# Attention over key tiles: one block of products per tile, four score banks, three single maxima banks

## The chip, the cores and the metric

The kernel runs on 1 core of one Trainium2 chip. The metric is the time of one execution in device microseconds (us); three runs were taken of the kernel before. The core's engines are named as in the profile: PE (TensorE, with its weight loads shown apart as PEld), DVE (VectorE), ACT (ScalarE), POOL (GpSimd) and SP (SyncE, which issues DMAs). Matmul results land in PSUM, eight banks of 128 partitions by 512 f32 numbers.

## The reference, cut to what matters

The whole reference is two transformer layers over 4096 tokens of width 256. The change touches the attention of the first layer alone: 16 heads of 16 numbers, every token against every token, with a bias linear in the distance.

```python
score = jnp.einsum('bhsd,bhnd->bhsn', q, k) / scale + bias[None]
attn = jax.nn.softmax(score, axis=-1)
out = jnp.einsum('bhsn,bhnd->bhsd', attn, v)
```

Behind it come a mixture of 64 experts, a second attention and a gated linear attention, each with its own stage in the kernel; they are the same in both versions.

## The kernel before, in words

`bias_attention` (from L663) walks over 8 chunks of 512 queries (c) and, in each, over 4 groups of 4 heads (g): 32 steps, each of 32 key tiles of 128 keys (k). A key tile makes three kinds of work.

- **Scores** (`score`, L1163 to L1171): for each of the 4 heads one matmul of 54 rows gives keys by queries, 128 x 512, into one of three banks `ps_exp`. ACT takes the exponential of each bank (`exps`, L831 to L837) into `probs`, which has two buffers of four heads.
- **Maxima**: the softmax needs each query's largest score before its exponentials are taken, so a step ahead of the scores PE makes the same products the other way round, queries by keys, for the *next* step (`unit_half`, L1139 to L1156). A unit is a pair of heads for 128 queries and 512 keys, two matmuls of 128 x 512; 64 units make a step, two go with each key tile. A unit fills a buffer of two banks, `ps_max0` or `ps_max1` in turn, and DVE reads the pair in one reduction of 128 x 1024 to 128 x 2 (L1100 in `units`). At the end of a step a short chain of DVE operations (L907 to L924) joins the maxima.
- **Products** (`products`, L1173 to L1188): probabilities times values, into one bank `ps_out`, four heads side by side in column groups of 32. They run one key tile behind the scores.

A score or a maxima matmul uses 54 of the array's rows, in its upper or lower half; one of each stand next to each other in PE's order, in opposite halves, and run side by side. A product uses all 128 rows and 32 columns, four heads side by side.

The order on PE is written by hand in `step` (L1217 on): for each half q of a key tile two scores and the two halves of one unit in turn, then the products of half the queries (256 columns).

```python
for q in range(2):
    for h in range(2):
        score(c, g, k, 2 * q + h)
        if ahead:
            mm = unit_half(c, g, d, u + q, 1 - h)
    ...
        products(c, g, k - 1, q)
```

The waits that matter: a unit's matmul waits until DVE has read the unit two before (semaphore `unit_read`, L1151); a score waits for the exponential three before (`exp_done`, L1169); the products of a tile wait for its four exponentials (L1177). The first 72 units (one step and 8 units) run before the first score. In the last step there is no unit to make, and in the step before it none for the last 4 tiles.

From the second chunk on, six pieces of the routing of the chunk before (`extra`, L1190 to L1215: transposes, router logits, ranks) are inserted on PE per chunk, behind the products of the tiles listed in EXTRA. Each takes one maxima buffer in turn, and ACT copies it out (L844 to L867). DVE's small operations of the routing stand between its reads of units (`pieces`, L1075). SP loads keys and values by counts of scores and products done (L739 to L754); POOL clears rows by counts of units read (L784).

Of the kernel before, what the change touches and what calls it, by code (L numbers as in the profile page):

```python
# [377 lines left out]
EB = 3  # L378
ROWS = 2 * NPR * BIAS * TC
EXPS = NT * HG  # L380
assert UNITS == 2 * NT and AHEAD % 2 == 0 and (NG * EXPS + 1) % EB == 0 and ROWS == P // 4
# [240 lines left out]
def extras_ahead(g, u):  # L622

    return sum(1 for xg, xk in EXTRA if xg < g or xg == g and unit_at(xk) < u)


def unit_place(c, g, d, u):

    ahead = g + d - 1
    if isinstance(c, int) and NG * c + ahead < 0:  # L630
        return u
    block, row = c + ahead // NG, ahead % NG
    place = UNITS * (NG * c + g + d) + u
    if isinstance(block, int) and block == 0:
        return place
    return place + len(EXTRA) * (block - 1) + extras_ahead(row, u)


def extra_place(c, i):

    g, k = EXTRA[i]
    return UNITS * (NG * c + g + 1) + unit_at(k) + 1 + len(EXTRA) * (c - 1) + i


def extra_behind(c, g, d, u, back):

    ahead = g + d - 1
    for i, (xg, xk) in enumerate(EXTRA):
        if c + ahead // NG >= 1 and xg == ahead % NG and unit_at(xk) + back == u:
            return i  # L650
    return None


def extra_buffer(i):

    return (unit_at(EXTRA[i][1]) + 1 + i) % 2
# [6 lines left out]
def bias_attention(nc, q_laid, k_laid, m_rows, v_aug, x_rows, y_rows, hT_rows, xres, mod, ident, r, slots, w_router, e_bias):  # L663

    with ExitStack() as ctx:
# [11 lines left out]
        ps_max = [pb(f"ps_max{i}", [P, 2, CH]) for i in range(2)]  # L677
# [19 lines left out]
        summed = lambda c, i: extra_place(c, i) + 1  # L697
        read = lambda c, i: len(EXTRA) * (c - 1) + i + 1

        with nc.Block() as block:  # L700
            @block.sync
            def _(sp):
# [34 lines left out]
                def step(c, g, last):  # L737

                    s = NG * c + g  # L739
                    for b in range(4):  # L740
# [6 lines left out]
                        if not (last and g == NG - 1):  # L747

                            hold(sp, pv_done, 2 * (NT * s + (b + 1) * QUART + 2), sp_passed)
                            load_vals((g + 1) % NG, b)  # L750
# [24 lines left out]
            def _(pool):  # L775
# [7 lines left out]
                for b in range(SLOTS // step_rows):  # L783
                    pool.wait_ge(unit_read, 2 + UNITS + 16 * (b + 1))  # L784
                    pool.dma_start(x_rows[b * step_rows:(b + 1) * step_rows, :].rearrange("(p r) d -> p r d", p=P),
                                   zeros[:, :].unsqueeze(1).to_broadcast([P, CLEAR_ROWS, PAY])).then_inc(cleared, 16)
# [43 lines left out]
            def _(act):  # L830
                def exps(s, g, k):  # L831

                    act.wait_ge(pv_done, 2 * (NT * s + k + 1))
# [5 lines left out]
                def copy_o(s, g):  # L839

                    act.wait_ge(pv_done, 2 * (NT * (s + 1) + 2))
                    act.activation(r.o[g][:, :], ps_out[:, :], ACT.Copy).then_inc(o_copied, 1)  # L842

                def copy_heads(c, i):  # L844
                    act.wait_ge(unit_summed, summed(c, HEADS + i))
                    act.wait_ge(heads_set, c - 1)
                    for half_ in range(2):
                        ps = ps_max[extra_buffer(HEADS + i)][:, half_, :].rearrange("p (h w) -> p h w", h=H0)
# [3 lines left out]
                def copy_turned(c, k):  # L852
                    act.wait_ge(unit_summed, summed(c, TURN + k))
                    act.activation(r.turned()[:, k, :], ps_max[extra_buffer(TURN + k)][:, 0, :],
                                   ACT.Copy).then_inc(extra_read, 1)

                def router_exp(c):
# [3 lines left out]
                                   ps_max[extra_buffer(LOGITS)][:, 0, 0:TC * E], ACT.Exp, scale=-1.0).then_inc(extra_read, 1)  # L861

                def copy_ranks(c):
# [3 lines left out]
                                   ps_max[extra_buffer(RANKS)][:, 0, :], ACT.Copy).then_inc(extra_read, 1)  # L867
# [33 lines left out]
            def _(dve):  # L901
# [3 lines left out]
                def maxima(s, i):  # L905
                    dve.wait_ge(unit_read, 2 + UNITS * (s + 1))
# [183 lines left out]
                def units(c, g, d, behind=True, first=False, link=None, span=range(UNITS)):  # L1090
# [3 lines left out]
                    for u in span:  # L1094
                        kb, row = divmod(u, TC * NPR)
                        tile, pair = divmod(row, NPR)
                        place = unit_place(c, g, d, u)
                        buffer = (u + (extras_ahead((g + d - 1) % NG, u) if link is not None else 0)) % 2
# [34 lines left out]
            def _(pe):  # L1133

                pe.sem_inc(unit_read, 2)
                pe.sem_inc(pv_done, 4)
                pe.sem_inc(exp_done, 2)

                def unit_half(c, g, d, u, h):  # L1139
# [8 lines left out]
                    place = unit_place(c, g, d, u)  # L1148
                    buffer = (u + extras_ahead((at - 1) % NG, u)) % 2 if not isinstance(place, int) else place % 2
                    behind, before_last = (extra_behind(c, g, d, u, back) for back in (1, 2))  # L1150
                    pe.wait_ge(unit_read, UNITS * (NG * c + at) + u + (1 if behind is None else 2))  # L1151
                    if before_last is not None:
                        pe.wait_ge(extra_read, read(c, before_last))
                    mm = pe.matmul(ps_max[buffer][:, h, :], quer[at % NG][half(h), pair, tile * P:(tile + 1) * P],  # L1154
                                   keys[at % 2][half(h), pair, kb * CH:(kb + 1) * CH], start=True, stop=True)
                    return mm  # L1156

                def unit(c, g, d, u):
                    for h in range(2):
                        mm = unit_half(c, g, d, u, h)  # L1160
                    mm.then_inc(unit_summed, 1)

                def score(c, g, k, j):  # L1163
# [5 lines left out]
                    pe.wait_ge(exp_done, EXPS * s + (n + 1 if g == 0 and n < 2 else n))  # L1169
# [3 lines left out]
                def products(c, g, k, q):  # L1173

                    s = NG * c + g
                    if q == 0:
                        pe.wait_ge(exp_done, EXPS * s + HG * (k + 1) + 2)  # L1177
                        if k % QUART == 0:
                            pe.wait_ge(v_loaded[k // QUART], 16 * (s + 1))
                        if k == 0:  # L1180

                            pe.wait_ge(o_copied, s)
# [1718 lines left out]
```

## Time and profile before

| what | value |
|---|---|
| median of 3 runs | 5146.05 us (5146.01 to 5150.23) |
| the profiled execution | 5163.93 us, span 5162.3 us |
| mean granted TensorE clock | 0.953 of full speed |
| PE busy | 4681.8 us, 91% of the span |
| DVE busy | 4057.1 us, 79% |
| ACT busy | 3071.8 us, 60% |
| POOL busy | 1114.2 us, 22% |

Every duration below is from that one profiled execution, which took 17.9 us more than the median. "Busy" is time in which at least one instruction of the engine was under way; matmuls are pipelined and their ends are modelled, so a busy PE is not PE at its peak, and two instructions that overlap count once. Weight loads (PEld) run beside the matmuls. In a timeline, a row that starts a little before the one ahead of it has ended is an overlap on the same engine.

### The profile page before, as it was taken

To read this page: it belongs to the slowest core of one execution; us is meant where nothing else is said; L and a number is where in the kernel's file an instruction comes from. 1 tells how busy PE (TensorE), PEld (TensorE's weight loads), DVE (VectorE), ACT (ScalarE), POOL (GpSimd) and SP (SyncE) were. 2 spreads that over 40 slices of the span, in tenths; PEclk is the share of its full clock that TensorE was granted. 3 is DMA by queue.
4 is the path that set the end of the run, shared out by engine and by line. 5 is a ranking of instruction groups with operands and counts; after the bars stand their busy time and mean duration, and the time that the engine had idled before them with its cause. 6 is when DMAs were issued, how large, how long until landed. Compare 5 with 4: busy or idle time off the path is not lost. (4 is left out here: it accounts for less than half of the span.)

```text
span 5162.3 us, 101254 instructions
## 1 busy us (share of the span) xinstructions
PE 4681.8 (91%) x39032; PEld 2403.0 (47%) x39032; DVE 4057.1 (79%) x5031; ACT 3071.8 (60%) x5309; POOL 1114.2 (22%) x1152
## 2 busy tenths in 40 slices
PE   5589999999999999999999888547899969999998
PEld 3233333333333333333333456425566646666666
DVE  4499999999999999999998233377765448788787
ACT  1158888888888888888888512112222225555554
POOL 0000012102121021211212210254320004444443
PEclk8679999999999999999999989879999979999999
DMA  5736545354443534444342137632110031111010
GB/s 181 165 87 156 137 75 114 67 90 90 80 81 71 89 72 89 78 75 85 67 86 53 33 107 224 202 95 79 60 55 4 11 125 31 28 27 29 25 29 17
DMA packets 242778, 421.66 MB, mean 82 GB/s; under 512 B 42569, under 2 KB 147034, under 8 KB 242256
## 3 DMA queue, kind: packets, MB, share of 16 engines
q1 hardware_dynamic: 195504, 341.87, 30.1%
q0 software_dynamic: 30048, 66.76, 4.1%
q10 hardware_dynamic: 16896, 8.39, 0.7%
q8 instruction: 236, 3.87, 0.3%
q14 instruction: 94, 0.77, 0.1%
HBM read 324.51 MB, written 129.17 MB: 88 GB/s over the span
## 5 line engine op out<-in xcount | busy, mean ns | idle before, releaser
L1100 DVE TENSOR_REDUCE attn_mpart<-attn_ps_max 128x2 f32<-128x1024 f32 x2048 | 2450.0, 1221 | 100.6 <-PE attn_ps_max L1154 95.0
L837 ACT ACTIVATE attn_probs<-attn_ps_exp 128x512 f32<-128x512 f32 x4096 | 2226.7, 595 | 315.0 <-PE attn_ps_exp L1170 231.4
L1154 PE MATMUL attn_ps_max<-attn_keys,attn_quer 54*128 54x512 f32 x4096 | 1481.4, 458 | 69.9 <-DMA attn_keys<-k_laid 37.9
L1170 PE MATMUL attn_ps_exp<-attn_quer,attn_keys 54*128 54x512 f32 x4096 | 1504.2, 447 | 0.2 <-ACT attn_probs L837 0.2
L1185 PE MATMUL attn_ps_out<-attn_probs,attn_vals 128*32 128x256 f32 x16384 | 1310.1, 391 | 9.8 <-ACT route_o L842 9.2
L1170 PEld LDWEIGHTS attn_ps_exp<-attn_quer,attn_keys 54*128 54x128 f32 x4096 | 616.2, 185 | 836.2 <-ACT attn_probs L837 781.4
L1185 PEld LDWEIGHTS attn_ps_out<-attn_probs,attn_vals 128*32 128x32 f32 x16384 | 323.4, 108 | 750.3 <-issue 394.9
L1154 PEld LDWEIGHTS attn_ps_max<-attn_keys,attn_quer 54*128 54x128 f32 x4096 | 591.7, 188 | 119.3 <-DVE attn_mpart L1100 75.9
L1724 POOL DMA_INDIRECT ra_rows<-y_rows,slots x256 | 252.8, 987 | 300.8 <-DVE ra_total L1892 227.0
L577 POOL DMA_INDIRECT x_rows<-route_pay,route_now x256 | 252.0, 984 | 299.9 <-DMA x_rows<-route_pay,route_now 213.0
L1856 ACT ACTIVATE ra_row<-ra_psS 128x512 f32<-128x512 f32 x112 | 66.9, 597 | 360.9 <-PE ra_psS L1777 360.9
L1796 PE MATMUL ra_psO<-ra_vals,ra_probT 128*128 128x256 f32 x1056 | 256.5, 388 | 7.8 <-DVE ra_probT L1972 7.8
L2379 POOL TENSOR_TENSOR gla_ke<-gla_kg,emask 128x512 f32<-128x512 f32 x128 | 152.2, 1217 | 514.7 <-DVE gla_kg L2605 514.7
L1777 PE MATMUL ra_psS<-ra_kT,ra_qT 128*128 128x512 f32 (+3 forms) x576 | 240.7, 573 | 6.6 <-DVE ra_kT L1942 6.6
L1796 PEld LDWEIGHTS ra_psO<-ra_vals,ra_probT 128*128 128x128 f32 x1056 | 198.9, 196 | 42.4 <-DVE ra_probT L1972 10.0
L2670 PE MATMUL gla_psP<-gla_wqkv,gla_hc 128*128 128x512 f32 x384 | 189.7, 631 | 2.5 <-ACT gla_egn L2459 2.0
L2464 ACT ACTIVATE gla_sq<-gla_psO 128x512 f32<-128x512 f32 x32 | 19.1, 597 | 266.4 <-PE gla_psO L2778 266.4
L2365 POOL TENSOR_TENSOR gla_qeT<-gla_ftT,gla_emr 128x512 f32<-128x512 f32 x128 | 173.1, 1385 | 14.0 <-ACT gla_ftT L2411 14.0
L1777 PEld LDWEIGHTS ra_psS<-ra_kT,ra_qT 128*128 128x128 f32 x576 | 109.2, 197 | 124.8 <-issue 114.3
L1594 DVE TENSOR_TENSOR exp_hidden<-exp_psU,exp_gate 128x256 f32<-128x256 f32 x64 | 27.2, 425 | 174.0 <-PE exp_psY L1647 144.1
L1972 DVE COPY ra_probT<-ra_psT 128x512 f32<-128x512 f32 (+2 forms) x144 | 90.2, 644 | 84.6 <-PE ra_psT L1787 83.7
L1892 DVE TENSOR_REDUCE ra_total<-ra_rows 128x256 f32<-128x2048 f32 x32 | 116.9, 3653 | 39.7 <-DMA ra_rows<-y_rows,slots 39.7
(390 smaller groups left out, 5346.8 us busy)
## 6 DMA issues: line engine op xcount, KB each, us to landing
attn_keys<-k_laid SPq DMA_DIRECT2D x256, 256.0 KB
attn_vals<-v_aug SPq DMA_DIRECT2D x128, 512.0 KB, 7.7
attn_keys<-k_laid SPq DMA_DIRECT2D x256, 128.0 KB
x_rows<-attn_zeros POOLq DMA_DIRECT2D x16, 1280.0 KB, 6.2
exp_x<-x_rows SPq DMA_DIRECT2D x64, 320.0 KB
exp_w1w<-in_w SPq DMA_DIRECT2D x64, 256.0 KB
y_rows<-exp_y SPq DMA_DIRECT2D x64, 256.0 KB
attn_keys<-k_laid SPq DMA_DIRECT2D x256, 48.0 KB
```

The source lines that it names most:

```text
L577: pool.indirect_dma_start(out=x_rows, out_offset=bass.IndirectOffsetOnAxis(ap=r.now[:, n, k:k + 1].bitcast(U32), axis=0), in_=r.pay[:, n, ...
L837: act.activation(probs[k % 2][:, j, :], ps_exp[bank_of(g, n)][:, :], ACT.Exp).then_inc(exp_done, 1)
L1100: dve.tensor_reduce(mpart[i][:, kb, TC * pair + tile::TC * NPR], ps_max[buffer][:, :, :], AX, ALU.max).then_inc(unit_read, 1)
L1154: mm = pe.matmul(ps_max[buffer][:, h, :], quer[at % NG][half(h), pair, tile * P:(tile + 1) * P], keys[at % 2][half(h), pair, kb * CH:(kb + ...
L1170: pe.matmul(ps_exp[bank_of(g, n)][:, :], keys[g % 2][half(h), pair, k * P:(k + 1) * P], quer[g][half(h), pair, :], start=True, stop=True). ...
L1185: mm = pe.matmul(ps_out[j * VW:(j + 1) * VW, n], vals[:, k, j * VW:(j + 1) * VW], probs[k % 2][:, j, n], start=(k == 0 and q == 0), stop=( ...
L1724: pool.indirect_dma_start(out=rows[n % 2][:, k, :], out_offset=None, in_=y_rows, in_offset=bass.IndirectOffsetOnAxis(ap=slots[:, n, k:k + ...
L1777: mm = pe.matmul(psS[g % 2][:, 0:width], qT[s // TC % 2][:, k, s % TC * P:(s % TC + 1) * P], kT[:, k, b * BLK:b * BLK + width], start=(k = ...
L1796: mm = pe.matmul(psO[s % 2][:, :], probT[(before(s) + b) % 2][:, j * P:(j + 1) * P], vals[:, n, :], start=(n == 0), stop=(n == s))
L2365: last = pool.tensor_tensor(qeT[:, b, :, :], ftT[:, 3, b, :].unsqueeze(1).to_broadcast([P, NE, P]), emr[i][:, :, :], ALU.mult)
L2379: last = pool.tensor_tensor(ke[i][:, e, :], kg2[:, :], emask[:, bass.ds(m, 1), e].to_broadcast([P, KDV]), ALU.mult)
L2670: mm = pe.matmul(ps, hc[i][:, k, :], wqkv[:, x, k, :], start=(k == 0), stop=(k == KD - 1))
```

## The change

All of it is in `bias_attention` and its helpers.

- The products of a key tile are one block of four matmuls of 512 columns behind all four scores and both units, in place of two blocks of four of 256 columns.
- The score banks become four (EB = 4), and a score waits for the exponential four before.
- The maxima's two buffers of two banks become a ring of three single banks (MB = 3). Each half of a unit takes the next bank, has its own count on `unit_summed` and `unit_read`, and DVE reads it alone: 128 x 512 to 128 x 1, twice as many reductions. A half waits until the half three places before has been read. The number of PSUM banks stays eight (3 + 4 + 1 for 4 + 3 + 1).
- A routing insert takes one or two places of the ring (two for the heads' transposes).

```diff
-EB = 3
+EB = 4
...
+EXTRA_BANKS = (2, 2, 1, 1, 1, 1)
+MB = 3
...
+def half_number(at, u, q):
+
+    return 2 * (UNITS * at + u) + q
+
+
+def half_place(at, u, q):
+
+    return half_number(at, u, q) + extras_before(at, u)[1]
...
-        ps_max = [pb(f"ps_max{i}", [P, 2, CH]) for i in range(2)]
+        ps_max = [pb(f"ps_max{i}", [P, CH]) for i in range(MB)]
...
-                        dve.wait_ge(unit_summed, place + 1)
-                        dve.tensor_reduce(mpart[i][:, kb, TC * pair + tile::TC * NPR], ps_max[buffer][:, :, :], AX,
-                                          ALU.max).then_inc(unit_read, 1)
+                        for q in range(2):
+                            dve.wait_ge(unit_summed, half_number(s, u, q) + extras_before(s, u)[0] + 1)
+                            at = TC * pair + tile + (1 - q) * TC * NPR
+                            dve.tensor_reduce(mpart[i][:, kb, at:at + 1], ps_max[half_place(s, u, q) % MB][:, :], AX,
+                                              ALU.max).then_inc(unit_read, 1)
...
+                def bank_free(place):
+                    if place - MB in EXTRA_PLACES:
+                        pe.wait_ge(extra_read, read(*EXTRA_PLACES[place - MB]))
+                    elif place >= MB:
+                        pe.wait_ge(unit_read, PLACES[place - MB] + 1)
...
-                    pe.wait_ge(unit_read, UNITS * (NG * c + at) + u + (1 if behind is None else 2))
...
-                    mm = pe.matmul(ps_max[buffer][:, h, :], quer[at % NG][half(h), pair, tile * P:(tile + 1) * P],
+                    place = half_place(NG * c + at, u, 1 - h)
+                    bank_free(place)
+                    mm = pe.matmul(ps_max[place % MB][:, :], quer[at % NG][half(h), pair, tile * P:(tile + 1) * P],
                                    keys[at % 2][half(h), pair, kb * CH:(kb + 1) * CH], start=True, stop=True)
-                    return mm
+                    mm.then_inc(unit_summed, 1)
...
-                    pe.wait_ge(exp_done, EXPS * s + (n + 1 if g == 0 and n < 2 else n))
+                    pe.wait_ge(exp_done, EXPS * s + n)
...
-                    n = slice(q * CH // 2, (q + 1) * CH // 2)
                     for j in range(HG):
-                        mm = pe.matmul(ps_out[j * VW:(j + 1) * VW, n], vals[:, k, j * VW:(j + 1) * VW],
-                                       probs[k % 2][:, j, n], start=(k == 0 and q == 0),
-                                       stop=(k == NT - 1 and q == 1), skip_group_check=True)
+                        mm = pe.matmul(ps_out[j * VW:(j + 1) * VW, :], vals[:, k, j * VW:(j + 1) * VW],
+                                       probs[k % 2][:, j, :], start=(k == 0), stop=(k == NT - 1), skip_group_check=True)
                     mm.then_inc(pv_done, 1)
...
-                        for q in range(2):
-                            for h in range(2):
-                                score(c, g, k, 2 * q + h)
-                                if ahead:
-                                    mm = unit_half(c, g, d, u + q, 1 - h)
...
+                        score(c, g, k, 0)
+                        if ahead:
+                            unit_half(c, g, d, u, 1)
+                        score(c, g, k, 1)
+                        if ahead:
+                            unit_half(c, g, d, u, 0)
+                        score(c, g, k, 2)
+                        if ahead:
+                            unit_half(c, g, d, u + 1, 1)
+                        score(c, g, k, 3)
+                        if ahead:
+                            unit_half(c, g, d, u + 1, 0)
+                        if k >= 1:
+                            products(c, g, k - 1)
```

The order on PE before, in the first chunk's second step: one key tile. `ps_exp` are score banks (L1170), `ps_max` the maxima's buffers of two banks (L1154), `ps_out` the products (L1185); the digits are buffer numbers.

```order
L1170 MATMUL attn_ps_exp1<-attn_quer1,attn_keys1 128x512
L1154 MATMUL attn_ps_max1<-attn_keys0,attn_quer2 128x512
L1170 MATMUL attn_ps_exp2<-attn_quer1,attn_keys1 128x512
L1154 MATMUL attn_ps_max1<-attn_keys0,attn_quer2 128x512
L1185 MATMUL attn_ps_out<-attn_probs1,attn_vals 32x256 x4
L1170 MATMUL attn_ps_exp0<-attn_quer1,attn_keys1 128x512
L1154 MATMUL attn_ps_max0<-attn_keys0,attn_quer2 128x512
L1170 MATMUL attn_ps_exp1<-attn_quer1,attn_keys1 128x512
L1154 MATMUL attn_ps_max0<-attn_keys0,attn_quer2 128x512
L1185 MATMUL attn_ps_out<-attn_probs1,attn_vals 32x256 x4
```

Each unit fills both banks of one buffer, and a block of products stands between any two units.

The order on PE with the change, at a key tile of the first chunk's third step (scores are now L1164, maxima L1149, products L1177; `ps_max0` to `ps_max2` are single banks).

```order
L1177 MATMUL attn_ps_out<-attn_probs1,attn_vals 32x512 x4
L1164 MATMUL attn_ps_exp0<-attn_quer2,attn_keys0 128x512
L1149 MATMUL attn_ps_max2<-attn_keys1,attn_quer3 128x512
L1164 MATMUL attn_ps_exp1<-attn_quer2,attn_keys0 128x512
L1149 MATMUL attn_ps_max0<-attn_keys1,attn_quer3 128x512
L1164 MATMUL attn_ps_exp2<-attn_quer2,attn_keys0 128x512
L1149 MATMUL attn_ps_max1<-attn_keys1,attn_quer3 128x512
L1164 MATMUL attn_ps_exp3<-attn_quer2,attn_keys0 128x512
L1149 MATMUL attn_ps_max2<-attn_keys1,attn_quer3 128x512
L1177 MATMUL attn_ps_out<-attn_probs0,attn_vals 32x512 x4
```

Between two blocks of products the first and the fourth maxima matmul now take the same bank, here `ps_max2`.

On DVE, before, reads of the two buffers alternate; with the change the reads walk through the three banks.

```order
L1094 TENSOR_REDUCE attn_mpart0<-attn_ps_max1 128x1
L1094 TENSOR_REDUCE attn_mpart0<-attn_ps_max2 128x1
L1094 TENSOR_REDUCE attn_mpart0<-attn_ps_max0 128x1
L1094 TENSOR_REDUCE attn_mpart0<-attn_ps_max1 128x1
L1094 TENSOR_REDUCE attn_mpart0<-attn_ps_max2 128x1
```

Each row is a reduction of one bank to one column, where L1100 took two banks to two columns.

## Rows read from the trace of the kernel before

**Rows 1.** Busy time by stretch: us, engines' busy us (instructions), granted clock, DMA.

```profile
222.00:302.00 80.00, 55.53 (x142) 20.45 (x140) 79.44 (x74) 0.00 (x0) 0.00 (x0) 0.50 0.59 105
303.00:2907.00 2604.00, 2586.83 (x24728) 979.24 (x24728) 2452.26 (x2494) 2260.46 (x4184) 428.67 (x472) 1.00 0.44 85
2835.00:2903.00 68.00, 67.44 (x608) 25.89 (x607) 0.00 (x0) 64.64 (x122) 15.69 (x16) 1.00 0.04 10
3000.00:3100.00 100.00, 78.33 (x298) 58.03 (x297) 29.34 (x70) 16.72 (x33) 0.72 (x1) 0.86 0.44 138
```

The engines' columns are, in this order, PE, PEld, DVE, ACT and POOL.

**Rows 2.** Groups by line: busy us, mean ns of one, idle before, its releaser.

```profile
L1100 DVE TENSOR_REDUCE attn_mpart<-attn_ps_max 128x2 f32<-128x1024 f32 x2048 | 2450.0, 1221 | 100.6 <-PE attn_ps_max L1154 95.0
L837 ACT ACTIVATE attn_probs<-attn_ps_exp 128x512 f32<-128x512 f32 x4096 | 2226.7, 595 | 315.0 <-PE attn_ps_exp L1170 231.4
...
L1170 PE MATMUL attn_ps_exp<-attn_quer,attn_keys 54*128 54x512 f32 x4096 | 1504.2, 447 | 0.2 <-ACT attn_probs L837 0.2
L1185 PE MATMUL attn_ps_out<-attn_probs,attn_vals 128*32 128x256 f32 x16384 | 1310.1, 391 | 9.8 <-ACT route_o L842 9.2
...
L1154 PEld LDWEIGHTS attn_ps_max<-attn_keys,attn_quer 54*128 54x128 f32 x4096 | 591.7, 188 | 119.3 <-DVE attn_mpart L1100 75.9
```

**Rows 3.** Timeline of the weight loads: start us, us, engine, line, operation, idle.

```profile
1499.64 0.18 PEld L1170 LDWEIGHTS attn_ps_exp<-attn_quer,attn_keys 54*128 54x128 f32 x1 [0.41 <-ACT attn_probs L837]
...
1500.87 0.18 PEld L1170 LDWEIGHTS attn_ps_exp<-attn_quer,attn_keys 54*128 54x128 f32 x1 [0.41 <-ACT attn_probs L837]
...
1501.54 0.16 PEld L1185 LDWEIGHTS attn_ps_out<-attn_probs,attn_vals 128*32 128x32 f32 x8 [0.37 <-issue]
1502.11 0.18 PEld L1170 LDWEIGHTS attn_ps_exp<-attn_quer,attn_keys 54*128 54x128 f32 x1 [0.41 <-ACT attn_probs L837]
...
1514.44 0.18 PEld L1170 LDWEIGHTS attn_ps_exp<-attn_quer,attn_keys 54*128 54x128 f32 x1 [0.41 <-ACT attn_probs L837]
```

**Rows 4.** Timeline of PE's matmuls in the same half tile.

```profile
1500.88 0.50 PE L1170 MATMUL attn_ps_exp<-attn_quer,attn_keys 54*128 54x512 f32 x1
...
1501.21 0.39 PE L1154 MATMUL attn_ps_max<-attn_keys,attn_quer 54*128 54x512 f32 x1
1501.22 0.39 PE L1170 MATMUL attn_ps_exp<-attn_quer,attn_keys 54*128 54x512 f32 x1
```

**Rows 5.** Timeline of DVE where a small operation stands between two reads.

```profile
819.41 1.23 DVE L1100 TENSOR_REDUCE attn_mpart<-attn_ps_max 128x2 f32<-128x1024 f32 x1 [0.86 <-PE attn_ps_max L1154]
820.55 0.16 DVE L1048 TENSOR_SCALAR route_wsum<-route_wsum 128x4 f32<-128x4 f32 x1
820.64 1.23 DVE L1100 TENSOR_REDUCE attn_mpart<-attn_ps_max 128x2 f32<-128x1024 f32 x1
```

**Rows 6.** Timeline of ACT and DVE in the half tile of rows 4.

```profile
1501.41 0.60 ACT L837 ACTIVATE attn_probs<-attn_ps_exp 128x512 f32<-128x512 f32 x1
...
1501.90 0.59 ACT L837 ACTIVATE attn_probs<-attn_ps_exp 128x512 f32<-128x512 f32 x1
...
1501.68 1.23 DVE L1100 TENSOR_REDUCE attn_mpart<-attn_ps_max 128x2 f32<-128x1024 f32 x1
```

**Rows 7.** Groups by line and shape: f32 matmuls of 256 and of 512 columns.

```profile
L1796 PE MATMUL ra_psO<-ra_vals,ra_probT 128*128 128x256 f32 x1056 | 256.5, 388 | 7.8 <-DVE ra_probT L1972 7.8
L1777 PE MATMUL ra_psS<-ra_kT,ra_qT 128*128 128x512 f32 x480 | 216.6, 605 | 6.6 <-DVE ra_kT L1942 6.6
```

**Rows 8.** DVE on 512 elements from PSUM: a group, and a timeline.

```profile
L2526 DVE TENSOR_REDUCE gla_kmx<-gla_psP 128x8 f32<-128x512 f32 x32 | 22.1, 692 | 65.5 <-PE gla_psP L2674 65.5
...
4252.76 0.69 DVE L2599 SCALAR_TENSOR_TENSOR gla_qg<-gla_psP,gla_eg 128x512 f32<-128x512 f32 x1 [0.95 <-PE gla_psP L2670]
4253.37 0.68 DVE L2605 TENSOR_TENSOR gla_kg<-gla_kx,gla_egn 128x512 f32<-128x512 f32 x1
```

**Rows 9.** Timeline in the prologue: a read, and the load that waited for it.

```profile
254.17 1.21 DVE L1100 TENSOR_REDUCE attn_mpart<-attn_ps_max 128x2 f32<-128x1024 f32 x1
...
255.44 0.29 PEld L1154 LDWEIGHTS attn_ps_max<-attn_keys,attn_quer 54*128 54x128 f32 x2 [0.84 <-DVE attn_mpart L1100]
```

More of the change, by code:

```diff
@@ L619, in unit_at, with extras_before, extra_place @@
     return AHEAD + 2 * k + 1
[L622 to L639, printed above, removed]
-    g, k = EXTRA[i]
[L642 to L656, printed above, removed]
+EXTRA_BANKS = (2, 2, 1, 1, 1, 1)
+MB = 3
+def extras_before(at, u):
+    done = [i for c in range(1, NC) for i, (g, k) in enumerate(EXTRA) if (NG * c + g + 1, unit_at(k)) < (at, u)]
+    return len(done), sum(EXTRA_BANKS[i] for i in done)
+def half_number(at, u, q):
+    return 2 * (UNITS * at + u) + q
+def half_place(at, u, q):
+    return half_number(at, u, q) + extras_before(at, u)[1]
+def extra_place(c, i, b):
+    g, k = EXTRA[i]
+    return half_place(NG * c + g + 1, unit_at(k), 1) + 1 + b
+PLACES = {half_place(at, u, q): half_number(at, u, q) for at in range(NG * NC) for u in range(UNITS) for q in range(2)}
+EXTRA_PLACES = {extra_place(c, i, b): (c, i) for c in range(1, NC) for i in range(len(EXTRA)) for b in range(EXTRA_BANKS[i])}
 DVE_LINKS, POOL_LINKS = 18, 19
@@ L1212, in extra @@
                         pe.wait_ge(mask_set, c)
[L1213 to L1214 removed]
+                        pe.matmul(ps[0][:, 0:TC * E], r.prior[:, :], r.maskb[:, :, :], start=True, stop=True)
+                        mm = pe.matmul(ps[0][:, TC * E:2 * TC * E], r.onesb[:, :], r.maskb[:, :, :], start=True, stop=True)
                     mm.then_inc(unit_summed, 1)
@@ L1224, in step @@
                         u %= UNITS
-                        for q in range(2):
-                            for h in range(2):
-                                score(c, g, k, 2 * q + h)
-                                if ahead:
-                                    mm = unit_half(c, g, d, u + q, 1 - h)
-                            if ahead:
-                                mm.then_inc(unit_summed, 1)
-                            if k >= 1:
-                                products(c, g, k - 1, q)
-                            elif not first:
-                                products(*before, NT - 1, q)
+                        score(c, g, k, 0)
[12 more added lines that the diff above has]
+                            products(c, g, k - 1)
+                        elif not first:
+                            products(*before, NT - 1)
                         if routing and (g, k) in EXTRA:
@@ L1251, in _ @@
                     step(NC - 1, g, left=min(2, NG - 1 - g))
-                for q in range(2):
-                    products(NC - 1, NG - 1, NT - 1, q)
+                products(NC - 1, NG - 1, NT - 1)
 def bias_constants():
```

65 lines of the change are left out of this document (28 added, 37 removed).

## The prediction, made before the changed kernel ran

> **What bounds the kernel now.** I read the table of stages first. Attention runs from 303 to 2907 us, 2604 of the 5162 us, at full TensorE clock, with PE busy 2587 and DVE 2452 of them [rows 1]. Only this stage is touched; what stands behind it just starts later. Next, the groups by line: 2048 reads of a pair of banks at 1221 ns, 4096 exponentials, 16384 product instructions at 391 ns (each product in the code is two of them) [rows 2]. Both PE and DVE look full, so the shares do not say which one sets the pace. One period of a key tile does.
>
> On PE's weight loads the scores' row returns at 1499.64, 1500.87 and 1502.11: half a tile is 1.23 us. Six tiles later it stands at 1514.44, so a tile takes 14.80 / 6 = 2.467 [rows 3]. Inside a half, with the matmul rows [rows 4]: loads at 1500.87; the pair of row-halves (score and maxima product side by side) ends 0.50 after its load began, 0.11 of that before its matmul proper (0.50 against the 0.39 of the next pair, whose weights were already in); the second pair starts at 1501.21 and 1501.22; the products' loads at 1501.54, 0.32 after it; the next scores' loads at 1502.11. These steps, 0.11 + 0.23 + 0.32 + 0.57, close the 1.23 without a stall. So PE sets the pace by its own sequence. The idle time that the load rows put down to ACT is idle of the loads while the matmuls still stream; matmuls of L1170 stood idle 0.2 us for it in all [rows 2].
>
> DVE is not the limit although it shows no gaps: near 820 us a small operation fits between two reads whose starts stay 1.23 apart (819.41 and 820.64); from a read's start to that operation's it is 1.14 [rows 5]. DVE thus needs about 2 x 1.14 = 2.28 of the 2.47. ACT needs 4 x 0.49 (starts at 1501.41 and 1501.90) = 1.96 [rows 6].
>
> **The change part by part.** I count a key tile: scores S0 to S3, maxima halves U0 to U3, then the products P.
>
> *Products in one block.* The two changes into P and the two back become one and one. Each change leaves about 0.1 of PE unused: a pair streams in 0.23 (0.11 + 0.23 gives the 0.34 from 1500.87 to 1501.21), and 0.32 passes before the products' loads, 0.09 to 0.11 more. P with 256 columns takes 0.57 from its loads to the next scores' [rows 3]. With 512 columns each of its two sets streams 256 columns longer, 0.21 by the mean of a 512-column against a 256-column matmul (605 and 388 ns) [rows 7], so P takes 0.57 + 2 x 0.21 = 0.99 to 1.00; if everything doubled it would be 1.14. PE alone would need 0.11 + 3 x 0.23 + 0.32 + 1.00 = 2.12 a tile: a gain of 0.35.
>
> *Reads of one bank.* Four instead of two. Nearest rows: a reduction of 512 elements from PSUM takes 692 ns, other operations on 512 from PSUM 0.68 to 0.69 [rows 8]; I take 0.685. Behind each other such operations start 0.60 to 0.61 apart (L2599 at 4252.76, L2605 at 4253.37) [rows 8], so DVE needs about 4 x 0.60 = 2.40, up from 2.28. That alone would still be below 2.47.
>
> The Trainium skill, page "VectorE: DVE Perf Modes", section on the TRN2 errata, prices a read from PSUM at 120 cycles plus its elements at 0.96 GHz; as an estimate by that page four reads cost 2.63 a tile, against the 2.40 of the rows. By it DVE would be the limit at 2.63, some 160 us slower than now. The rows' 0.61 decides: the second started 0.08 before the first was over.
>
> *The ring of three.* This is the term that decides. Before, a unit's load waits for the unit two back, whose read began a half tile or more earlier. Now U3 takes the bank of U0 **of the same tile**, and P is queued behind U3 on PE, and the next tile's U0 behind P. That closes a loop:
> - U0: loads to the end of its matmul 0.50 [rows 4];
> - to DVE's start 0.07 to 0.08: 1501.21 + 0.39 = 1501.60, read at 1501.68 [rows 4, 6];
> - the read 0.685 [rows 8];
> - end of read to PE's waiting load 0.05 to 0.06: 254.17 + 1.21 = 255.38, load at 255.44 [rows 9];
> - U3: load to matmul 0.11, then 0.32 to the products' loads: 0.43 [rows 3, 4];
> - P: 1.00.
>
> Sum 0.50 + 0.075 + 0.685 + 0.055 + 0.43 + 1.00 = **2.74 us** a tile, above PE's 2.12 and DVE's 2.40. All of PE's gain is eaten, and 0.27 more. DVE is idle 0.34 a tile while it happens, and PE about 0.36 (from U2's end, 0.11 + 2 x 0.23 + 0.39 = 0.96 after the first load, to U3's load at 0.50 + 0.075 + 0.685 + 0.055 = 1.32).
>
> Tiles with maxima beside the scores: 31 steps of 32 less the last 4 = 988. 988 x (2.74 - 2.467) = **+270**.
>
> *Four score banks.* A score waits for the exponential four back instead of three. PE's matmuls lose 0.2 us to that wait now [rows 2], so nothing is won beside the maxima. In the last 36 tiles, which have no maxima, ACT does 122 instructions in 68 us, 2.23 a tile [rows 1]; PE's and ACT's own needs there are under 2.0, so up to 0.2 each: **-7**.
>
> *Wait for the copied output.* 9.2 us of PE [rows 2] are lost where the first products of a step wait for ACT's copy. They now stand at the tile's end, later than the copy: **-9**.
>
> *Prologue.* 72 units without scores, DVE-bound (79.4 of 80 us busy) [rows 1], at 80 / 72 = 1.1 a unit; now 2 x 0.60, so 72 times 0.06 to 0.1: **+5**.
>
> *Routing inserts and step ends.* The stage's 2604 us are 1024 x 2.467 = 2526 and 78 more, for six inserts a chunk and the maxima's chain at step ends. An insert takes one or two of three banks and holds them until ACT has copied, as it held one of two pairs; on the other side DVE's small pieces fall into its 0.34 of idle. I take no change, and a third of 78 either way, 26. The thresholds of SP's and POOL's waits name the same events as before, so no transfer moves against its tile.
>
> Sum: 270 - 7 - 9 + 5 = **+259**, say +257 with the roundings. The profiled execution took 5163.9, 17.9 above the median of the three runs. 5163.9 + 257 - 17.9 = **5403 us**, 5.0% slower. A measurement of this kernel can tell 0.2%, about 10 us, from no change.
>
> **The rivals.**
> - *Faster: the ring never stops PE.* It decides at U3's load: if U0 has been read by the time three pairs are through, 0.11 + 3 x 0.23 = 0.80 after U0's load, DVE's 2.40 becomes the pace and the gain of the single block shows. 988 x (2.40 - 2.467) = -66, with about 26 given back by routing pieces that DVE could no longer hide, -40 with the small terms: some 5105. Against it: by the rows the bank is free 0.50 + 0.08 + 0.69 + 0.06 = 1.33 after that load, half a microsecond late. The Trainium skill, page "TensorEngine Tiling (Array Packing)", section "Key Properties", says that changing the tiling mode drains TensorE; by that rule halving the changes must pay, as here. The trace agrees on the cost, some 0.1 a change [rows 3, 4], but not on what limits once the ring is there. Chance 0.06.
> - *About the same.* Loop and gain cancel within 10 us, if the loop is 2.47. No row gives that; 0.03.
> - *Slower still: the block costs double.* P at 1.14 makes the loop 2.88: 5403 + 988 x 0.14 = 5541. Against it, the 217 ns between 256 and 512 columns. Chance 0.05.
> - *Slower still: the clock.* PE idles 0.36 of 2.74 in each tile, 13%. A stretch with PE busy 78% was granted 0.86, one at 99% 1.00 [rows 1]. At 0.95 PE's 1.93 of the loop grow by 0.10: about 5500. Chance 0.05.
>
> **How the numbers follow.** The ring's loop at 2.74 has the remaining 0.81, and its time is the forecast. Its own bounds: a read of 0.655 to 0.69, the two waits and roundings 0.03 either way, the inserts 26 us: 5403 - 60 and + 60. The range, 5335 to 5465, holds most of that case and leaves out the rivals, together under 2 in 10. Slower by over 0.2%: 0.91 (three cases); within: 0.03; faster: 0.06.
>
> **What would show it.** In the changed profile: 4096 reads of about 685 ns, DVE busy near 2800 us in them; 8192 product instructions near 600 ns; tile period 2.74, attention some 255 us longer at clock 1.00; and, as the mark of the ring, the maxima's loads waiting for DVE's reads, about a third of a microsecond once a tile, 300 us or more in all (now 75.9 [rows 2]). I am wrong if that wait is absent, or if it is there and the period still is 2.47 or less.

## The result, and the profile after

The changed kernel takes **5395.28 us** (median of 4 runs, 5391.15 to 5400.45) against 5146.03 us (median of 4, 5140.71 to 5150.23): a ratio of 1.0485, interval 1.0467 to 1.0504. The forecast was 5403, 0.14% above. The profiled execution took 5395.94 us, 232 more than the profiled one of before.

Those 232 us lie between the first and the last score, which are 2601.1 us apart before and 2838.1 after: +237. The first score came 4.1 us earlier, what follows the last was 0.9 shorter, and 237.0 - 4.1 - 0.9 = 232.0. Behind the 4.1 are two things: the first unit began 9 us earlier, in a part that the change does not touch (over the eight profiled executions of this document it begins between 212.5 and 221.5 us), and the prologue, from the first unit to the first score, took 86.8 us in place of 81.9.

The table of stretches of the changed kernel (us, then PE, PEld, DVE, ACT and POOL busy, granted clock, DMA share, GB/s), answering to [rows 1]: the prologue, the attention stage (the last score is at 3137, so this stretch has some 22 us of what follows), and a part of the last step.

```profile
212.00:299.00 87.00, 85.36 (x144) 40.57 (x145) 85.53 (x146) 0.00 (x0) 0.00 (x0) 0.50 0.57 102
303.00:3160.00 2857.00, 2750.86 (x16564) 1104.89 (x16562) 2548.31 (x4490) 2152.24 (x4186) 429.35 (x474) 1.00 0.40 78
3074.00:3134.00 60.00, 59.92 (x348) 19.55 (x348) 0.00 (x0) 58.73 (x118) 14.69 (x15) 1.00 0.04 11
```

In the second stretch PE is busy 2751 of 2857 us (2741 of 2839 from the first score to the last), where it was busy 2587 of 2604, and the clock is still 1.00, so it is not the clock that took the time. DVE is busy 89% where it was 94%, with more instructions. The shares alone would call this a kernel bound by PE still, at 96%; one tile, below, says otherwise. In the last step, without maxima, PE is full: from the first score of its first tile to that of its last, 31 tiles, it takes 64.5 us, 2.08 a tile, where it took 70.0, 2.26 a tile.

The groups by line, answering to [rows 2]:

```profile
L1094 DVE TENSOR_REDUCE attn_mpart<-attn_ps_max 128x1 f32<-128x512 f32 x4096 | 2541.7, 681 | 256.0 <-PE attn_ps_max L1149 251.1
L831 ACT ACTIVATE attn_probs<-attn_ps_exp 128x512 f32<-128x512 f32 x4096 | 2114.2, 604 | 634.8 <-PE attn_ps_exp L1164 632.5
...
L1177 PE MATMUL attn_ps_out<-attn_probs,attn_vals 128*32 128x512 f32 x8192 | 1092.1, 605 | 0.7 <-ACT attn_probs L831 0.6
L1149 PEld LDWEIGHTS attn_ps_max<-attn_keys,attn_quer 54*128 54x128 f32 x4096 | 695.6, 188 | 639.5 <-DVE attn_mpart L1094 584.1
```

A read now takes 681 ns, a product instruction 605 ns, and there are half as many products. The last row is the one to look for: the maxima's loads wait 584 us for DVE's reads, and waited 75.9 before; without the prologue it is 541 against 20. In the other direction DVE waits 251 us for the maxima's matmuls. Two engines that wait for each other in every tile are what a loop would leave; the experiments test it.

One tile, on the weight loads (start us, us, engine, line, operation, idle before it and what ended that), answering to [rows 3]:

```profile
1505.07 0.18 PEld L1164 LDWEIGHTS attn_ps_exp<-attn_quer,attn_keys 54*128 54x128 f32 x1 [0.84 <-ACT attn_probs L831]
1505.08 0.29 PEld L1149 LDWEIGHTS attn_ps_max<-attn_keys,attn_quer 54*128 54x128 f32 x2
...
1506.38 0.18 PEld L1149 LDWEIGHTS attn_ps_max<-attn_keys,attn_quer 54*128 54x128 f32 x1 [0.55 <-DVE attn_mpart L1094]
1506.81 0.16 PEld L1177 LDWEIGHTS attn_ps_out<-attn_probs,attn_vals 128*32 128x32 f32 x8 [0.24 <-ACT attn_probs L831]
1507.80 0.18 PEld L1164 LDWEIGHTS attn_ps_exp<-attn_quer,attn_keys 54*128 54x128 f32 x1 [0.84 <-ACT attn_probs L831]
```

and on PE and DVE in the same tile (timelines of their own):

```profile
1505.08 0.50 PE L1149 MATMUL attn_ps_max<-attn_keys,attn_quer 54*128 54x512 f32 x1
...
1505.64 0.62 PE L1164 MATMUL attn_ps_exp<-attn_quer,attn_keys 54*128 54x512 f32 x2
...
1506.38 0.49 PE L1149 MATMUL attn_ps_max<-attn_keys,attn_quer 54*128 54x512 f32 x1
```

```profile
1505.64 0.69 DVE L1094 TENSOR_REDUCE attn_mpart<-attn_ps_max 128x1 f32<-128x512 f32 x1 [0.25 <-PE attn_ps_max L1149]
```

Go round once. U0's matmul begins at 1505.08 and ends at 1505.57 (the rows are rounded); DVE, which had been idle for 0.25 us, starts its read at 1505.64 and ends it at 1506.33; U3's load stands ready and starts at 1506.38; the products' loads follow 0.43 later; the next tile begins 0.99 after them. From 1505.07 to 1507.80 it is 2.73 us. Of the two long idle times in the load rows only one is a stall: the 0.84 ahead of a tile's first score is the loads' own idleness while the products still stream, the 0.55 ahead of U3 is PE standing before DVE. For the most of it PE is not even idle in the profile: S2 and S3 go on until 1506.26 (the row of two at 1505.64), and only 0.12 is left without a matmul. But S3 runs by itself there and U3 by itself behind it, where the two would have run side by side in 0.23. This is how a tile can lose 0.27 us with PE busy 96%.

### The profile page after: what moved, and what is told of

Read it like the earlier page. It is cut to its first block and busy times, and to the rows that moved or that the text cites. A ratio compares the mean times of both kernels' runs of the same rounds, so it can differ in the third digit from the quotient of the medians.

```text
span 5394.3 us, 86833 instructions
## 1 busy us (share of the span) xinstructions
PE 4862.2 (90%) x30840; PEld 2539.4 (47%) x30840; DVE 4150.0 (77%) x7079; ACT 2962.8 (55%) x5309; POOL 1114.6 (21%) x1152
## 5 line engine op out<-in xcount | busy, mean ns | idle before, releaser
L1094 DVE TENSOR_REDUCE attn_mpart<-attn_ps_max 128x1 f32<-128x512 f32 x4096 | 2541.7, 681 | 256.0 <-PE attn_ps_max L1149 251.1
L831 ACT ACTIVATE attn_probs<-attn_ps_exp 128x512 f32<-128x512 f32 x4096 | 2114.2, 604 | 634.8 <-PE attn_ps_exp L1164 632.5
L1149 PE MATMUL attn_ps_max<-attn_keys,attn_quer 54*128 54x512 f32 x4096 | 1571.1, 462 | 134.7 <-DMA attn_keys<-k_laid 36.1
L1164 PE MATMUL attn_ps_exp<-attn_quer,attn_keys 54*128 54x512 f32 x4096 | 1256.7, 420 | 0.1
L1164 PEld LDWEIGHTS attn_ps_exp<-attn_quer,attn_keys 54*128 54x128 f32 x4096 | 676.5, 185 | 896.4 <-ACT attn_probs L831 802.2
L1177 PE MATMUL attn_ps_out<-attn_probs,attn_vals 128*32 128x512 f32 x8192 | 1092.1, 605 | 0.7 <-ACT attn_probs L831 0.6
L1149 PEld LDWEIGHTS attn_ps_max<-attn_keys,attn_quer 54*128 54x128 f32 x4096 | 695.6, 188 | 639.5 <-DVE attn_mpart L1094 584.1
L1177 PEld LDWEIGHTS attn_ps_out<-attn_probs,attn_vals 128*32 128x32 f32 x8192 | 161.3, 108 | 250.8 <-ACT attn_probs L831 235.9
L1968 DVE COPY ra_probT<-ra_psT 128x512 f32<-128x512 f32 (+2 forms) x144 | 90.1, 643 | 84.6 <-PE ra_psT L1783 83.8
```

The lines of the kernel that those rows point to most:

```text
L831: act.activation(probs[k % 2][:, j, :], ps_exp[bank_of(g, n)][:, :], ACT.Exp).then_inc(exp_done, 1)
L1094: dve.tensor_reduce(mpart[i][:, kb, at:at + 1], ps_max[half_place(s, u, q) % MB][:, :], AX, ALU.max).then_inc(unit_read, 1)
L1149: mm = pe.matmul(ps_max[place % MB][:, :], quer[at % NG][half(h), pair, tile * P:(tile + 1) * P], keys[at % 2][half(h), pair, kb * CH:(kb ...
L1164: pe.matmul(ps_exp[bank_of(g, n)][:, :], keys[g % 2][half(h), pair, k * P:(k + 1) * P], quer[g][half(h), pair, :], start=True, stop=True). ...
L1177: mm = pe.matmul(ps_out[j * VW:(j + 1) * VW, :], vals[:, k, j * VW:(j + 1) * VW], probs[k % 2][:, j, :], start=(k == 0), stop=(k == NT - 1 ...
```

## The experiments

Two theories beside the ring's loop could give the same slowdown: that four single reads are simply too much for DVE (throughput, with no part for the ring), and that the one block is dearer on PE than two. The first four experiments take one of these away each: the ring's shortness, the one block, a half and three quarters of the read. Each is timed against runs of the kernel before on the same chip. None of the six times fell inside its expected range (experiment 2 missed it by 1 us), so what each experiment decides is read from its tile period and its waits.

### Experiment 1: a ring of four, paid with a score bank

The changed kernel with four maxima banks and three score banks.

```diff
-EB = 4
+EB = 3
...
-MB = 3
+MB = 4
...
-    return (EXPS * g + n) % EB
+    return (EXPS * s + n) % EB
```

> The changed kernel with the banks dealt the other way: four for the maxima, three for the scores (4 + 3 + 1). Loop theory: U3 takes another bank than U0, so the loop through DVE's read is gone, and the longest closed path is now the scores': S0 0.50, 0.04 to ACT, exponential 0.60, 0.05 back, S3 0.43, products 1.00 = 2.62 a tile. 988 tiles x (2.62 - 2.73) = -110: 5285 us (5255 to 5315), and PE's loads wait for ACT once a tile in place of DVE. Rival 1, four single reads are DVE's limit: the tile stays at 2.73 and the time at 5395. Rival 2, the 512-column block itself is dear: no change, 5395. Rival 3, only the maxima's ring held it and DVE's 2.40 is next: 5070.

Measured: 5378.91 us, ratio 1.0428 (1.0395 to 1.0461). The wait for DVE went as the loop theory wants, but the time did not: an expectation missed by 94 us, and by the time alone this run is nearer to rivals 1 and 2 (5395). The waits decide against rival 1; rival 2 is left to experiments 3 and 4. Waits of the weight loads between 900 and 2900 us (total us, times, longest):

```profile
PEld attn_ps_exp L1164 <- ACT attn_probs L831: 1077.4, 1414, 1.0
...
PEld attn_ps_max L1149 <- DVE attn_mpart L1094: 7.2, 32, 0.3
```

Not all of the first row is a stall: in each tile 0.84 of it is the loads' own idleness while the products stream, as in the changed kernel. The stall is the 0.71 ahead of S3. A tile takes 2.67, by the loads and ACT's timeline:

```profile
1507.41 0.18 PEld L1164 LDWEIGHTS attn_ps_exp<-attn_quer,attn_keys 54*128 54x128 f32 x1 [0.84 <-ACT attn_probs L831]
1508.65 0.18 PEld L1164 LDWEIGHTS attn_ps_exp<-attn_quer,attn_keys 54*128 54x128 f32 x1 [0.71 <-ACT attn_probs L831]
1509.08 0.16 PEld L1177 LDWEIGHTS attn_ps_out<-attn_probs,attn_vals 128*32 128x32 f32 x8 [0.24 <-ACT attn_probs L831]
1510.08 0.18 PEld L1164 LDWEIGHTS attn_ps_exp<-attn_quer,attn_keys 54*128 54x128 f32 x1 [0.84 <-ACT attn_probs L831]
```

```profile
1508.01 0.60 ACT L831 ACTIVATE attn_probs<-attn_ps_exp 128x512 f32<-128x512 f32 x1 [0.59 <-PE attn_ps_exp L1164]
```

It is the same loop with ACT in DVE's place. With three score banks S3 takes the bank of S0 of its own tile: matmul 0.50, 0.10 until ACT starts, exponential 0.60, 0.04 to S3's load at 1508.65, 0.43 to the products, 1.00 for them, 2.67 in all. The expectation had put this loop at 2.62 by a shorter way to ACT; 988 tiles by 0.044 (median tile 2.664) are 43 us of the miss. About 60 more are in the last step, and the ends of the steps give some of that back. Stretches, columns as above, the second within the last step:

```profile
900.00:2900.00 2000.00, 1805.52 (x12032) 649.32 (x12034) 1884.90 (x3347) 1549.37 (x3015) 333.31 (x357) 1.00 0.41 76
...
3005.00:3115.00 110.00, 101.64 (x323) 26.08 (x315) 0.00 (x0) 54.71 (x106) 10.79 (x11) 0.50 0.01 1
```

There the granted clock is at 0.50, the lower of its two levels (1.2 GHz), a tile takes 4.13 and the step 124.7 us, against 64.5 in the changed kernel, whose last step kept 1.00. The expectation had left out the last step in two ways. The scores' loop goes on there without the maxima: as long as the clock was still 1.00 a tile took 2.66 (loads at 2994.68, 2997.34 and 3000.00), which over 31 tiles is 18 us more than 2.08. The rest is the clock.

### Experiment 2: the products in two blocks again

The changed kernel with its order of before: ring of three, single reads, four score banks, but products in two blocks of 256 columns.

```diff
                         score(c, g, k, 1)
                         if ahead:
                             unit_half(c, g, d, u, 0)
+                        block(0)
                         score(c, g, k, 2)
...
-                        if k >= 1:
-                            products(c, g, k - 1)
-                        elif not first:
-                            products(*before, NT - 1)
+                        block(1)
```

> The changed kernel with the products back in two blocks of 256 columns, one behind each pair of scores; ring of three and four score banks kept. Loop theory: between U0 and U3 there is a block of products, so U0's bank is read by the time U3 comes, PE sets the pace by its own sequence as before, tile 2.47. What is left of the ring is the prologue (+5) and the routing inserts (0 to +50): 5175 us (5145 to 5205). Rival 1, single reads cost by themselves: at 2.63 a tile or more, 5300 and up. Rival 2, the block itself was what cost: 5146, as the loop theory.

Measured: 5205.78 us, ratio 1.0086 (1.0059 to 1.0114), just above the upper edge of what was expected. The tile is back at 2.47 (loads of a tile's first score; then the reads' group, and the waits between 900 and 2900 us):

```profile
1500.49 0.18 PEld L1164 LDWEIGHTS attn_ps_exp<-attn_quer,attn_keys 54*128 54x128 f32 x1 [0.41 <-ACT attn_probs L831]
...
1502.96 0.18 PEld L1164 LDWEIGHTS attn_ps_exp<-attn_quer,attn_keys 54*128 54x128 f32 x1 [0.41 <-ACT attn_probs L831]
```

```profile
L1094 DVE TENSOR_REDUCE attn_mpart<-attn_ps_max 128x1 f32<-128x512 f32 x4096 | 2515.7, 681 | 89.3 <-PE attn_ps_max L1149 87.6
```

```profile
PEld attn_ps_max L1149 <- DVE attn_mpart L1094: 37.6, 116, 1.1
```

The same 4096 reads of 681 ns through the same three banks now fit into 2.47 us a tile. So neither the number of reads nor the ring alone makes the kernel slow; it is the ring of three *and* the one block. What this kernel still costs over before stands mostly in its three kinds of routing steps: 85.9, 85.8 and 82.3 us (82.5, 83.8 and 80.9 before), 6.7 a chunk and 47 in seven chunks; the prologue has 5. Part of it is the ring: in the first kind, after each of two inserts, a maxima's load waits until ACT has copied the insert out, and the tile takes 0.6 longer, 1.2 of the 3.4:

```profile
977.48 0.18 PEld L1149 LDWEIGHTS attn_ps_max<-attn_keys,attn_quer 54*128 54x128 f32 x1 [0.55 <-ACT attn_raw L843]
```

Most of the other extra time stands in tiles with small operations of the routing on DVE. With four reads a tile DVE has 0.07 of 2.47 to spare, so these pieces would no longer fit in; that is argued, and no run separates it.

### Experiments 3 and 4: shorter reads

The changed kernel, its reads cut to the last 256 and to the last 128 of a bank's 512 keys.

```diff
-ps_max[half_place(s, u, q) % MB][:, :], AX,
+ps_max[half_place(s, u, q) % MB][:, 256:], AX,
```

(`384:` in experiment 4.)

> The changed kernel, but DVE reads only the last 256 of the 512 columns of each maxima bank (the maxima then come from half of the keys). Loop theory: the read stands once in the loop; 256 elements at 0.96 GHz are 0.27, so the tile falls from 2.73 to 2.47: 988 x 0.267 = -264, 5131 us (5105 to 5160). Rival 1, DVE's four reads set the pace: four times 0.27 come off until PE's 2.12 stops it, 5395 - 600 = 4790. Rival 2, the block: no change, 5395.

> As the run with 256 columns, with the last 128 columns of each bank read (maxima from a quarter of the keys). Loop theory: the read is 0.40 shorter, tile 2.73 - 0.40 = 2.33, below the 2.47 of the kernel before, since the gain of the single block (PE's own 2.12) comes into the open: 5395 - 395 = 5000 us (4965 to 5035). Rival 1, DVE's pace: 4790, as with 256. Rival 2, the block itself costs: no change, 5395; and if the block gives no gain, not under 5130.

Measured: 5088.16 us, ratio 0.9865 (0.9834 to 0.9896), and 4956.91 us, ratio 0.961 (0.9578 to 0.9642). Both are some 43 us faster than expected, and both tiles are as expected. Reads of 256, one tile on the loads, and the group:

```profile
1502.83 0.18 PEld L1164 LDWEIGHTS attn_ps_exp<-attn_quer,attn_keys 54*128 54x128 f32 x1 [0.84 <-ACT attn_probs L831]
...
1503.88 0.18 PEld L1149 LDWEIGHTS attn_ps_max<-attn_keys,attn_quer 54*128 54x128 f32 x1 [0.29 <-DVE attn_mpart L1094]
1504.31 0.16 PEld L1177 LDWEIGHTS attn_ps_out<-attn_probs,attn_vals 128*32 128x32 f32 x8 [0.24 <-ACT attn_probs L831]
1505.30 0.18 PEld L1164 LDWEIGHTS attn_ps_exp<-attn_quer,attn_keys 54*128 54x128 f32 x1 [0.84 <-ACT attn_probs L831]
```

```profile
L1094 DVE TENSOR_REDUCE attn_mpart<-attn_ps_max 128x1 f32<-128x256 f32 x4096 | 1483.4, 418 | 1001.0 <-PE attn_ps_max L1149 996.4
```

Reads of 128, likewise (the last load belongs to a routing insert, which stands at the next tile's beginning):

```profile
1504.99 0.18 PEld L1164 LDWEIGHTS attn_ps_exp<-attn_quer,attn_keys 54*128 54x128 f32 x1 [0.84 <-ACT attn_probs L831]
...
1505.90 0.18 PEld L1149 LDWEIGHTS attn_ps_max<-attn_keys,attn_quer 54*128 54x128 f32 x1 [0.15 <-DVE attn_mpart L1094]
1506.32 0.16 PEld L1177 LDWEIGHTS attn_ps_out<-attn_probs,attn_vals 128*32 128x32 f32 x8 [0.24 <-ACT attn_probs L831]
1507.32 0.75 PEld L1191 LDWEIGHTS attn_ps_max<-ident,route_o 128*128 128x128 f32 x7 [0.84 <-DVE attn_mpart L1094]
```

```profile
L1094 DVE TENSOR_REDUCE attn_mpart<-attn_ps_max 128x1 f32<-128x128 f32 x4096 | 1069.4, 290 | 1271.5 <-PE attn_ps_max L1149 1175.8
```

This is the plainest evidence. The read goes from 681 to 418 to 290 ns, the tile from 2.733 to 2.467 to 2.333: 0.26 and 0.13 less of one, 0.27 and 0.13 less of the other. A tile gets shorter by **one** read's shortening, although it has four reads; were DVE's throughput the limit, it would be four times that, until another limit stopped it. With reads of 256 DVE is idle for 1001 us and a tile still takes what it took before the change. What the two expectations forgot is the prologue, where in the changed kernel DVE was busy 85.5 of 87 us and which shorter reads shorten too (63.8 and 57.2 us in place of 86.8), and the ends of steps, where a shorter read also shortens the maxima's tail: a plain step (one without routing) takes 78.93 with reads of 256, 32 x 2.467 and nothing more, where the changed kernel's takes 0.57 more than 32 of its tiles.

### Experiment 5: both

Ring of four, three score banks, and reads of 256: the edits of experiments 1 and 3 together.

```diff
-MB = 3
+MB = 4
...
+ps_max[half_place(s, u, q) % MB][:, 256:], AX,
```

> Four maxima banks and three score banks, and DVE reads only the last 256 columns of each maxima bank (maxima from half of the keys). Loop theory: the limit there is the scores' loop through ACT, 2.62 a tile, in which no DVE read stands: the same as four banks with whole reads, within 15 us, some 5285. Rival, DVE's reads or its waits still set the pace: faster by up to 988 x 0.27 = 264.

Measured: 5342.24 us, ratio 1.0362 (1.0311 to 1.0414), 37 us less than experiment 1, where 15 were allowed for. The median tile is 2.664, the same to three figures as with whole reads: DVE's read is not in that loop at all. S3's loads in two tiles:

```profile
1505.24 0.18 PEld L1164 LDWEIGHTS attn_ps_exp<-attn_quer,attn_keys 54*128 54x128 f32 x1 [0.71 <-ACT attn_probs L831]
...
1507.90 0.18 PEld L1164 LDWEIGHTS attn_ps_exp<-attn_quer,attn_keys 54*128 54x128 f32 x1 [0.71 <-ACT attn_probs L831]
```

In the profiles the two kernels differ by 34 us, and 31 of these are the prologue's, 54.8 us in place of 86.2. The last step is slow here too, 127.9 us (columns as above):

```profile
2970.00:3085.00 115.00, 106.22 (x336) 27.30 (x335) 0.00 (x0) 57.59 (x112) 7.16 (x8) 0.50 0.01 4
```

### Experiment 6: the kernel before, with one block

Three score banks, two pairs for the maxima and one reduction of two banks as before; only the products are one block.

```diff
-                            if k >= 1:
-                                products(c, g, k - 1, q)
-                            elif not first:
-                                products(*before, NT - 1, q)
+                        if k >= 1:
+                            products(c, g, k - 1)
+                        elif not first:
+                            products(*before, NT - 1)
```

> The kernel before (two pairs of maxima banks read two at a time, three score banks), with nothing changed but the products of a tile in one block of 512 columns. Loop theory: S3 takes S0's bank in the same tile, loop S0 - exponential - S3 - products at 2.62 a tile (a pair's read binds at about the same length): 5146 + 988 x (2.62 - 2.467) = 5297 us (5265 to 5330). Rival, the block is a gain and only the single-bank ring spoiled it: PE's 2.12 and DVE's 2.28 a tile would give 5146 - 988 x 0.19 = 4960. Rival, the block itself costs: 5395 or more.

Measured: 5385.63 us, ratio 1.0447 (1.0377 to 1.0516); expected too low for the same reasons as experiment 1: the scores' loop is 2.668 a tile (median), and the last step takes 118.7 us. One tile on the loads, waits between 900 and 2900 us (0.84 a tile of the row is again no stall), and a stretch of the last step:

```profile
1500.24 0.18 PEld L1170 LDWEIGHTS attn_ps_exp<-attn_quer,attn_keys 54*128 54x128 f32 x1 [0.84 <-ACT attn_probs L837]
...
1501.49 0.18 PEld L1170 LDWEIGHTS attn_ps_exp<-attn_quer,attn_keys 54*128 54x128 f32 x1 [0.51 <-ACT attn_probs L837]
...
1502.92 0.18 PEld L1170 LDWEIGHTS attn_ps_exp<-attn_quer,attn_keys 54*128 54x128 f32 x1 [0.84 <-ACT attn_probs L837]
```

```profile
PEld attn_ps_exp L1170 <- ACT attn_probs L837: 887.8, 1344, 0.8
```

```profile
3012.00:3120.00 108.00, 98.05 (x340) 25.72 (x336) 0.00 (x0) 58.04 (x113) 11.73 (x12) 0.56 0.01 4
```

So the one block loses with the banks as they were, too. Between two blocks of products each of the two rings has four uses, and each split tried with one block leaves one ring with three: scores in experiments 1, 5 and 6, maxima in the change. Four and four with the output's bank would be nine of eight, so a kernel without either loop was not run. No kernel run with whole reads beat the one before.

## Why the prediction was right

- **The loop** was predicted from six rows as 0.50 + 0.075 + 0.685 + 0.055 + 0.43 + 1.00 = 2.74. The trace after has 0.50, 0.07, 0.69, 0.05, 0.43, 0.99. That it is a loop, and not DVE's throughput, is shown by experiments 3 and 4; that it needs the one block, by experiment 2; that it needs the ring of three, by the waits of experiment 1, though not by its time. An undisturbed tile takes 2.733 us, and took 2.46 in most stretches before (2.467 in the one that the prediction read): 0.27 more, as predicted. Two rows of scores and one of products of the kernel before, on PE (the first products of a step are in the last row):

```profile
387.12 0.49 PE L1170 MATMUL attn_ps_exp<-attn_quer,attn_keys 54*128 54x512 f32 x1
...
389.58 0.50 PE L1170 MATMUL attn_ps_exp<-attn_quer,attn_keys 54*128 54x512 f32 x1
...
390.61 0.64 PE L1185 MATMUL attn_ps_out<-attn_probs,attn_vals 128*32 128x256 f32 x8 [0.29 <-ACT route_o L842]
```

  A plain step takes 88.04 us where it took 79.55, 8.49 more: 32 x 0.273, less 0.36 for the copied output, and 0.13 more at its end.
- **The price of the single block** was right: 0.99 for a block, no doubling, clock 1.00 in the stage. These two rivals fall by the trace itself. That the block does save PE time is seen where the loop is shortened or absent: 2.33 a tile in experiment 4, and 2.08 in the last step. PE's 2.12 beside the maxima was reached by no run.
- **DVE's pace.** The rows gave 0.60 from one read's start to the next, 2.40 for four. A single read takes 681 ns, and experiment 2 does four in each tile of 2.47, so the rows decide. By the figures of the Trainium skill, page "VectorE: DVE Perf Modes", the section on the TRN2 errata, one read is an estimate of 658 ns and four are 2.63 us: near the length of a single read, and too high as a pace for reads behind one another.
- **Small terms.** The prologue was predicted at +5 and took 4.9 more. The wait for the copied output went, as forecast (0.7 us of idle before the products, 9.8 in [rows 2]; 0.36 a step). The last 36 tiles, from their first score to the last, take 73.3 us where they took 80.2: 6.9 less, forecast 7, but not by the four score banks alone, to which the prediction put it down. Experiment 2 has these too, and its last 36 tiles take 80.1 us, its last step 65 / 116 x 4 = 2.24 a tile:

```profile
2890.00:2955.00 65.00, 59.96 (x586) 19.91 (x587) 0.00 (x0) 62.15 (x116) 13.71 (x14) 1.00 0.03 7
```

  With one block and three score banks it is 2.66 (experiment 1, before the clock fell), so the gain takes both. The inserts were put at no change and are some 2.2 us a chunk cheaper: the three kinds of routing steps exceed three plain ones by 6.4 us together, 8.6 before, 15 us in seven chunks. That DVE's idle time in each tile takes up the pieces is the likely reason; it was only argued.
- **How near it came.** The medians differ by 249 us, the forecast had 257. In the two profiles it is 241 without the different start, 16 under the forecast, and about 15 of these are the inserts, put at nothing. That the total lies within 0.14% of the measured time is in part luck.
- **Marks.** The wait for DVE's reads was called at 300 us or more and is 584, since the row counts 0.55 a tile, from the end of S3's load, where I had counted 0.36 of idle PE. That idleness was a wrong picture: S3 stands ahead of U3 and fills most of it, so PE's idle time is 98 us in the stage, 0.12 in the tile shown. DVE's, put at 0.34 a tile, is 0.25. The rival of the clock rested on this idleness of 13%, and was weaker than I put it. DVE's busy time in the reads was called near 2800 and is 2542: 4096 x 681 ns is 2790, but the reads overlap, and an overlap counts once. Neither entered the sum. Two slips in the prediction did not either: the faster rival's 5105 is 5095 with the small terms that it names (-66 + 26 - 11), and the lower bound of 0.655 for a read stands in none of its rows, which give 0.68 to 0.69.

The rival that the ring never stops PE was decided where the prediction said, at U3's load: 1.30 us after U0's, half a microsecond after three pairs would have been through. By the prediction's estimate PE's own sequence, with the gain of the block, would have been shorter than before by 0.35 (the most that a run beside the maxima showed is 0.13, in experiment 4, where the loop still holds); the loop made the tile longer by 0.27.

## What to carry to other kernels

In this kernel a ring of buffers cost time when it held fewer uses than stand between two points where an engine that works in order does something else: if a use late in a group waits for an early one of the **same** group, the producer's pass, the consumer's start and read, and all that is queued behind the late use add up to a loop, whatever the engines' totals say. Write that loop out piece by piece from the trace and compare it with each engine's own need; when the loop wins, making the consumer's single operation shorter pays once per loop (experiments 3 and 4). By the same account a better pace of the consumer, with each operation as long as before, would pay nothing; no run here tried that. Before merging blocks on the producer, count the uses between two blocks for every ring that the producer feeds, not only for the one that the change touches.

## What the runs showed that I had not expected

- **The clock in the last step.** With one block and three score banks the granted clock fell to 0.50 (experiments 1, 5 and 6; the 0.56 of experiment 6 is the mean of a stretch that began at 1.00) in tiles without maxima. A tile then takes 4.13, where the same loop took 2.66 at 1.00. The last step is 54 to 63 us longer than in the changed kernel, about 18 of it the loop and the rest the clock; I had priced this loop with the clock unchanged. In the kernel before and in the change the same step kept 1.00, with PE busy 67.4 of 68 and 59.9 of 60 us. In experiment 1 PE had been busy 1805.5 of 2000 us at 1.00 while the maxima ran beside the scores. After them the loop was the same, 2.66 a tile, and PE was busy 3.97 of 5 us (2995 to 3000), still at 1.00, before the clock fell. What exactly makes it fall no run separates.
- **A read's length and a read's pace are two numbers.** A reduction of 512 from PSUM is 681 ns long, but behind another it starts 0.60 after it; in a loop the first counts, for throughput the second. Mixing them up would have made this loop 0.08 too short, or DVE's need 0.33 a tile too long.
- **The way to ACT.** In the changed kernel and in experiment 1, ACT's first exponential of a tile starts 0.10 after the end of the score's matmul; in the kernel before it was 0.04 in rows 4 and 6 (1501.37 to 1501.41), as the expectation had it. DVE's read of a maximum starts 0.07 after the matmul.
